# Channel mix of a four-layer block: LayerNorm output transposed by DMA in fp16 halves instead of by TensorE

## Chip, cores and metric

The kernel runs on one core of a Trainium2 chip. The metric is the device time of one execution in microseconds (us), the median of several runs.

## What is computed

A residual stream `x` of 8 sequences (batches) of 512 tokens and 512 features passes through four layers: a cosine cross attention, a ternary feed-forward network, a softmax cross attention, and a channel mix. The change touches only the last one, which adds to `x` the following function of its layer norm:

```python
x_prev = jnp.concatenate([jnp.zeros((B, 1, C), x.dtype), x[:, :-1, :]], axis=1)
xr = mu_r * x + (1.0 - mu_r) * x_prev
xk = mu_k * x + (1.0 - mu_k) * x_prev
r = jax.nn.sigmoid(jnp.einsum('btc,dc->btd', xr, W_r))
k = jnp.einsum('btc,dc->btd', xk, W_k)
k_act = jnp.square(jax.nn.relu(k))
out = r * jnp.einsum('btc,dc->btd', k_act, W_v)
```

Here `x` is the layer norm (no gain, no bias) of the stream, and `x_prev` is the same one token earlier. All products are taken in fp16 with a high and a low half for each operand, three matmuls for one product, so that the result is close to float32.

## The kernel before

The stream stays in SBUF for the whole program (`X`, 128 tokens on the partitions, four token tiles a batch). The four stages run one after the other; the channel mix (`channel_mix`, from L1867) is the last. In it each engine has a program of its own, written out by hand: a first batch, a loop over batches 1 to 6 (`batches`), and a last one. Semaphores are wrapped in `Tally`, so that `s.wait(e, b, k)` waits until k signals of batch b are there. An engine executes its program strictly in order.

While batch b is multiplied, batch b+1 is prepared:

- **VectorE** (`step`, L2021): statistics (L135), `bn_aggr`, the normalised tokens `z` (L147, after GpSimd's 1/sqrt at L161), then eight mixed rows `xf` (L2007, `mix`): four that feed the keys, and then four that feed the gates, each of these ahead of `gated` (L2014, `y` = values times gate) and `add` (L2019) of one token tile of batch b.
- **TensorE** (`step`, L2077): `keys(b)`, 4 x 12 matmuls; `ln_t`, which turns `z` of batch b+1 by 16 float32 transposes (L165), four for each 128-feature chunk, into two PSUM banks; `gates(b)`, 4 x 12 matmuls; `values(b)`, 4 x 12 matmuls. `values` of token tile 2 waits until `y` of tile 0 has freed its bank (L2072).
- **ScalarE** (`step`, L1981): for the keys a Relu, a Square and a copy to fp16 (L1969 to L1974); `transposed`, four copies of 128x512 from PSUM into `zf` (features on the partitions, tokens along them, one zero column first, L1946); then `part` (L1954, the previous-token term) and `xh` (L1962, the fp16 high half of a mixed row), with the four sigmoids (`gate`, L1979) between them.
- **GpSimd** (`step`, L1928): 1/sqrt, four low halves of the squared keys `kl` (L1926), and eight low halves of the mixed rows `xl` (L1920).
- **SyncE**: one store of 1 MB a batch (L1908).

The first key matmul of batch b+1 needs the four `xl` of the keys, the first gate matmul all eight.

Of the kernel before, what the change touches and what calls it, by code (L numbers as in the profile page):

```python
# [14 lines left out]
P = 128  # L15
# [14 lines left out]
class Tally:  # L30

    def __init__(self, sem, per, by=1):
        self.sem, self.per, self.by = sem, per, by

    def count(self, b, k):

        return b * (self.per * self.by) + k * self.by + 1

    def wait(self, eng, b, k):

        n = self.count(b, k)
        if isinstance(n, int) and n <= 1:
            return
        eng.wait_ge(self.sem, n)  # L46
        if not isinstance(n, int) and eng.engine in (mybir.EngineType.Pool, mybir.EngineType.DVE, mybir.EngineType.SP):
            eng.nop(nofuse=True)  # L48


def starts():


    each = lambda names, value: {n: value for n in names.split()}
    norm = lambda batch: each("st mv z", 1 + batch * TT) | each("ve rstd", 1 + batch) | each("T", 1 + batch * KD)
    a = each("hi lo bias const ws wp wm wt raw0 raw1", 0) | norm(0) | each(
        "x cf zh zl ch cl proj pf sq ph pl norm root rec nmr dot w y add", 1)
# [5 lines left out]
    m = each("hi lo raw", 0) | norm(1) | each("zf", 1 + KD) | each("part xf xh xl", 1 + KD) | each(  # L63
        "kp kf kk kh kl rp r vp y x out", 1)
    return dict(a=a, f=f, s=s, m=m)


def program(nc, x_d, ctx_d, wv_d, bv_d, wt_d, bt_d, w1_d, cw_d, cb_d, w2_d,
            wq_d, bq_d, wk_d, bk_d, wvv_d, bvv_d, wo_d, bo_d, wr_d, wkk_d, wvo_d, mur_d, muk_d, out_d):
    with ExitStack() as ctx:  # L70
# [7 lines left out]
        def tile(b, q):  # L78

            return X[:, bass.ds(b * (TT * D) + q * D, D)]  # L80

        sems = {stage: {n: ctx.enter_context(nc.semaphore(f"{stage}_{n}")) for n in names}
                for stage, names in starts().items()}
        env = dict(nc=nc, X=X, ident=ident, ones=ones, mhalf=mhalf, banks=banks, pairs=pairs, tile=tile, sems=sems)
        sm = lambda n, shape, dt=F32: ctx.enter_context(nc.sbuf_tensor("sm_" + n, shape, dt))
        env.update(zz=sm("zz", [P, 2 * KD * (S + 1)], F16), cx=sm("cx", [P, 4 * KD * S], F16),
# [1780 lines left out]
def channel_mix(env, wvo_d, out_d):  # L1867
# [3 lines left out]
    with ExitStack() as ctx:  # L1871
# [15 lines left out]
        T, KB, RB, VB = banks[0:2], banks[2:4], banks[4:6], banks[6:8]  # L1887

        s_hi, s_lo = sem("hi"), sem("lo")
        s_raw = [sem("raw")]  # L1890
        s_zf = tally("zf", KD)
# [4 lines left out]
        ln_v, ln_p, ln_t, s_T, s_z = norm_tools(env, a, sem, tally)  # L1896
# [4 lines left out]
        @block.sync  # L1901
        def _(e):
            ws(e)

            def store(b):
                s_x.wait(e, b, TT)
                s_out.wait(e, b, 0)
                e.dma_start(out_d[bass.ds(b, 1), :, :].rearrange("o (q p) d -> p (o q) d", p=P),  # L1908
                            X[:, bass.ds(b * (TT * D), TT * D)].rearrange("p (q d) -> p q d", d=D))\
                    .then_inc(s_out.sem, 16)  # L1910
            store(0)
            batches(e, 1, B, store)
            s_out.wait(e, B, 0)

        @block.gpsimd
        def _(e):
            def mixed(b, first=0):
                for i in range(first, 2 * KD):
                    s_xh.wait(e, b, i + 1)
                    e.tensor_tensor(xl[:, i, :], xf[:, i % 3, :], xh[:, i, :], ALU.subtract).then_inc(s_xl.sem, 1)  # L1920

            def squared(b):
                s_vp.wait(e, b, 0)
                for m in range(KD):
                    s_kh.wait(e, b, m + 1)
                    e.tensor_tensor(kl[:, m, :], kk[:, m % 3, :], kh[:, m, :], ALU.subtract).then_inc(s_kl.sem, 1)  # L1926

            def step(b, last):  # L1928
                if not last:
                    ln_p(e, b + 1)  # L1930
                squared(b)
                if not last:
                    mixed(b + 1)

            mixed(0, KD)
            step(0, False)
            batches(e, 1, B - 1, lambda b: step(b, False))
            step(B - 1, True)

        @block.scalar  # L1940
        def _(e):
            def transposed(b):
                s_xf.wait(e, b, 0)
                for c in range(KD):
                    s_T.wait(e, b, c + 1)
                    e.activation(zf[:, c, 1:S + 1], T[c % 2][:, :], ACT.Copy).then_inc(s_zf.sem, 1)  # L1946

            def mix(b, i, begun=0):

                if i < 2 * KD:  # L1950
                    c = i % KD
                    s_zf.wait(e, b, c + 1)
                    s_xf.wait(e, b, max(i - 1, begun))
                    e.activation(part[:, i % 2, :], zf[:, c, 0:S], ACT.Copy, scale=omu[:, i:i + 1])\  # L1954
                        .then_inc(s_part.sem, 1)
                if i > begun:
                    if i == 1:
                        s_kp.wait(e, b, 0)
                    if i == KD + 1:
                        s_rp.wait(e, b, 0)  # L1960
# [3 lines left out]
            def keys(b):  # L1964
                s_vp.wait(e, b, 0)
                for m in range(KD):
                    s_kk.wait(e, b, max(m - 1, 0))
                    s_kp.wait(e, b, m + 1)
                    e.activation(kf[:, m % 2, :], KB[m % 2][:, :], ACT.Relu, scale=1 / WS).then_inc(s_kf.sem, 1)  # L1969
                    s_kf.wait(e, b, m + 1)  # L1970
                    s_kl.wait(e, b, max(m - 2, 0))
                    e.activation(kk[:, m % 3, :], kf[:, m % 2, :], ACT.Square).then_inc(s_kk.sem, 1)  # L1972
                    s_kk.wait(e, b, m + 1)
                    e.activation(kh[:, m, :], kk[:, m % 3, :], ACT.Copy).then_inc(s_kh.sem, 1)  # L1974

            def gate(b, q):
                s_y.wait(e, b, 0)
                s_rp.wait(e, b, q + 1)
                e.activation(r[:, q, :], RB[q % 2][:, :], ACT.Sigmoid, scale=1 / WS).then_inc(s_r.sem, 1)  # L1979

            def step(b, last, first=False):  # L1981
                keys(b)
                if not last:
                    transposed(b + 1)
                if first:
                    wa(e)
                for q in range(TT):
                    if not last:
                        mix(b + 1, q)
                    gate(b, q)  # L1990
                if not last:
                    for i in range(TT, 2 * KD + 1):
                        mix(b + 1, i)

            for i in range(KD, 2 * KD + 1):
                mix(0, i, KD)
            step(0, False, True)
            batches(e, 1, B - 1, lambda b: step(b, False))
            step(B - 1, True)

        @block.vector
        def _(e):
            def mix(b, i):
# [37 lines left out]
        def _(e):  # L2041
# [85 lines left out]
```

## Time and profile before

| | |
|---|---|
| median of 3 runs | 1653.15 us (1650.3 to 1653.52) |
| the profiled execution | 1648.01 us, of which its span 1646.2 us |
| channel mix in it | from 1360.6 us to the end |
| one batch of it, start of keys to start of the next keys | 35.09 us |

The profile gives for one execution how long each engine was busy, what released it after a wait, and when each instruction started. A batch is the stretch from its first key matmul (1467.96 us for the batch shown below) to the next one's.

### The profile page before, as it was taken

How to read it: one execution, taken by the hardware profiler on the slowest of the kernel's cores; microseconds unless marked ns; L12 is line 12 of the kernel's file. 1: busy time of each engine (PE TensorE's matmuls, PEld its weight loads, DVE VectorE, ACT ScalarE, POOL GpSimd, SP SyncE). 2: the span in 40 equal slices, each digit the busy share in tenths (PEclk: the TensorE clock that was granted, in tenths of full speed). 3: DMA queues.
4: the chain of work that ended last, by engine and by line, in shares of the span. 5: the costliest groups of instructions: out<-in, count | busy, mean ns of one | idle time of the engine just before them, and what ended most of it. 6: DMA issues, size and time to landing. Idle time of an engine off the chain costs nothing. (4 is left out here: it accounts for less than half of the span.)

```text
span 1646.2 us, 28592 instructions
## 1 busy us (share of the span) xinstructions
PE 1495.9 (91%) x8836; PEld 672.5 (41%) x8836; DVE 1189.8 (72%) x1438; ACT 1116.6 (68%) x1895; POOL 1022.6 (62%) x738
## 2 busy tenths in 40 slices
PE   5989888998999984889999999999999969999998
PEld 3545433443444441334333434343434314444443
DVE  4989898988888764667686868676777756555562
ACT  6677598887888752667666767666766656666662
POOL 4777537766777732766677767677767565454442
PEclk9999999999999996999999999999999979999999
DMA  8321000000000023121121212121211200100001
GB/s 327 132 77 51 0 1 1 1 1 1 0 1 1 22 64 89 35 55 39 42 55 38 58 34 58 35 57 35 57 35 40 56 26 26 52 25 25 25 25 51
DMA packets 61225, 72.16 MB, mean 44 GB/s; under 512 B 15312, under 2 KB 40784, under 8 KB 60624
## 3 DMA queue, kind: packets, MB, share of 16 engines
q1 hardware_dynamic: 57968, 62.36, 12.9%
q10 hardware_dynamic: 3168, 8.78, 1.4%
q8 instruction: 36, 0.59, 0.2%
q14 instruction: 53, 0.43, 0.1%
HBM read 37.40 MB, written 8.39 MB: 28 GB/s over the span
## 5 line engine op out<-in xcount | busy, mean ns | idle before, releaser
L1607 DVE TENSOR_REDUCE s_mx<-bank 128x2 f32<-128x1024 f32 x256 | 301.0, 1218 | 176.0 <-PE bank L1733 175.2
L1483 ACT ACTIVATE s_E<-bank 128x512 f32<-128x512 f32 x512 | 281.5, 597 | 165.3 <-PE bank L1751 164.2
L1367 POOL TENSOR_TENSOR s_E<-s_E 128x1024 f32<-128x1024 f32 x128 | 302.7, 2376 | 79.8 <-ACT s_E L1483 79.0
L1751 PE MATMUL bank<-s_QA,s_KA 97*128 97x512 f16 x512 | 164.7, 385 | 21.6 <-DMA s_QA<-s_mrow 10.8
L1920 POOL TENSOR_TENSOR sm_cx<-m_xf,sm_cx 128x512 f16<-128x512 f32 x60 | 84.1, 1408 | 102.1 <-ACT sm_cx L1962 102.1
L1759 PE MATMUL bank<-s_E,s_V 128*32 128x512 f32 x1024 | 138.5, 613 | 4.8 <-ACT s_E L1483 2.9
L1611 DVE RECIPROCAL bank<-bank 128x256 f32<-128x256 f32 (+1 forms) x66 | 112.7, 1707 | 17.6 <-PE bank L1767 17.6
L1112 PE MATMUL bank<-f_w2q,w2raw 128*128 128x512 f16 x512 | 121.8, 379 | 0.6 <-DVE w2raw L964 0.3
L1089 PE MATMUL bank<-sm_zz,w1raw 128*128 128x512 f16 x256 | 100.6, 393 | 23.6 <-DVE sm_cx L976 13.4
L786 POOL TENSOR_TENSOR sm_wkv<-sm_wkv,sm_cx 128x511 f32<-128x511 f32 x48 | 66.2, 1379 | 89.0 <-DVE sm_wkv L976 79.6
L780 POOL TENSOR_TENSOR w1raw<-w1raw,sm_cx 128x512 f32<-128x512 f32 x88 | 115.8, 1338 | 2.3 <-ACT sm_cx L868 2.3
L2007 DVE SCALAR_TENSOR_TENSOR m_xf<-sm_zz,sm_mu,m_part 128x512 f32<-128x512 f32 x60 | 58.6, 978 | 75.9 <-ACT m_part L1954 74.9
L1089 PE MATMUL bank<-sm_wq,w1raw 128*128 128x512 f16 x256 | 97.2, 380 | 12.0 <-DVE sm_cx L976 7.7
L1090 PE MATMUL bank<-sm_zz,w1raw 128*128 128x512 f16 x256 | 100.3, 392 | 0.0
L1090 PE MATMUL bank<-sm_wq,w1raw 128*128 128x512 f16 x256 | 97.0, 379 | 0.0
L1751 PEld LDWEIGHTS bank<-s_QA,s_KA 97*128 97x128 f16 x512 | 41.1, 97 | 121.6 <-DVE s_mx L1607 72.4
L1360 POOL TENSOR_TENSOR sm_cx<-s_qkf,sm_cx 128x512 f16<-128x512 f32 x32 | 37.1, 1159 | 80.4 <-ACT sm_cx L1461 80.0
L1112 PEld LDWEIGHTS bank<-f_w2q,w2raw 128*128 128x128 f16 x512 | 49.9, 98 | 61.3 <-ACT w2raw L926 0.8
L1767 PE MATMUL bank<-s_E,ones 128*32 128x512 f32 x512 | 69.0, 612 | 5.3 <-POOL s_E L1367 5.3
L1360 POOL TENSOR_TENSOR sm_cx<-s_qkf,s_qkh 128x512 f16<-128x512 f32 x32 | 37.1, 1160 | 56.0 <-ACT s_qkh L1461 54.3
L1694 PE MATMUL bank<-sm_wkv,sm_cx 128*128 128x128 f16 x384 | 69.7, 220 | 0.8 <-DVE sm_wkv L197 0.8
L1696 PE MATMUL bank<-sm_wkv,sm_cx 128*128 128x128 f16 x384 | 69.3, 219 | 0.0
(268 smaller groups left out, 4031.3 us busy)
## 6 DMA issues: line engine op xcount, KB each, us to landing
sm_cx<-in_ctx SPq DMA_DIRECT2D x16, 768.0 KB, 4.6
X<-in_x SPq DMA_DIRECT2D x8, 1024.0 KB, 6.3
s_QA<-sm_cx SPq DMA_DIRECT2D x256, 32.0 KB, 1.9
out_x<-X SPq DMA_DIRECT2D x8, 1024.0 KB, 4.3
s_KA<-sm_cx SPq DMA_DIRECT2D x244, 32.0 KB, 1.9
w1raw<-in_w ACTq DMA_DIRECT2D x1, 4096.0 KB, 14.2
w2raw<-in_w ACTq DMA_DIRECT2D x1, 4096.0 KB, 27.2
s_QA<-s_qkh SPq DMA_DIRECT2D x128, 32.0 KB, 1.9
```

Of the source, the lines that this page charges most:

```text
L780: e.tensor_tensor(o, o, s2b[:, :], ALU.mult).then_inc(s_u.sem, 1)
L1089: e.matmul(hb(odd, j), w1q[:, cols], zh(odd, c), start=(c == 0), stop=False)
L1090: last = e.matmul(hb(odd, j), w1q[:, cols], zl(odd, c), start=False, stop=(c == KD - 1))
L1112: last = e.matmul(OB[q][:, :], whole16[:, r % NQ, q * P:(q + 1) * P, 0], w2q[:, ORDER[r] * D:(ORDER[r] + 1) * D], start=False, stop=(r == ...
L1360: e.tensor_tensor(qkl[:, w, :], qkf[:, :], qkh[m % 2][:, w, :], ALU.subtract).then_inc(s_qkl.sem, 1)
L1367: e.tensor_tensor(into, into, other, ALU.add).then_inc(s_sum.sem, 1)
L1483: e.activation(E[:, SLOT[k] + h, :], s_bank(u, nxt)[:, :], ACT.Exp, scale=1.0 / float(np.sqrt(DH)))\
L1607: e.tensor_reduce(mx[:, 2 * i:2 * i + 2, q], MAXED[i][:, :, :], AX.X, ALU.max).then_inc(s_red.sem, 1)
L1611: e.reciprocal(DEN[:, i * n:(i + 1) * n], DEN[:, i * n:(i + 1) * n]).then_inc(s_rc.sem, 1)
L1751: e.matmul(s_bank(u, nxt)[:, :], KA[0:MROW + 1, m, h, t * P:(t + 1) * P], QA[0:MROW + 1, m, h, :], start=True, stop=True).then_inc(s_sc.se ...
L1759: e.matmul(NUM[h * DH:(h + 1) * DH, :], V[:, m, t, h * DH:(h + 1) * DH], E[:, SLOT[t] + h, :], start=(t == 0), stop=(t == TT - 1)).then_in ...
L1920: e.tensor_tensor(xl[:, i, :], xf[:, i % 3, :], xh[:, i, :], ALU.subtract).then_inc(s_xl.sem, 1)
```

## The change

`z` is no longer transposed by TensorE. VectorE still writes it in float32. ScalarE copies each token tile to fp16 (`zth`), two tiles after key 2 and two after key 3; VectorE subtracts (`ztl = z - zth`); SyncE issues for each token tile two DMA transposes, of 128 tokens x 512 features in fp16, 128 KB each, SBUF to SBUF; and GpSimd adds the two turned halves into `zf` for one token tile at a time (`joined`). So `zf` is complete for any feature chunk only when all four token tiles are in; `mix` now waits for all four (`s_zf.wait(e, b, TT)`). ScalarE's four copies out of PSUM are gone, and its first `part` moves from ahead of gate 0 to behind gate 1. `values` and its wait for `y` are as they were. Six of the added counters use semaphores of the first stage again, from the value where that stage left them.

```diff
@@ sync @@
+            def transposed(b):
+                for q in range(TT):
+                    cols = slice(q * P, (q + 1) * P)
+                    s_zth.wait(e, b, q + 1)
+                    e.dma_start_transpose(zTh[:, :, cols], zth[:, q, :]).then_inc(s_zT[q].sem, 16)
+                    s_ztl.wait(e, b, q + 1)
+                    e.dma_start_transpose(zTl[:, :, cols], ztl[:, q, :]).then_inc(s_zT[q].sem, 16)
+            def step(b, last):
+                if not last:
+                    transposed(b + 1)
+                store(b)
@@ gpsimd @@
+            def joined(b):
+                s_xf.wait(e, b, 0)
+                for q in range(TT):
+                    s_zT[q].wait(e, b, 2)
+                    cols = slice(q * P, (q + 1) * P)
+                    e.tensor_tensor(zf[:, :, 1 + q * P:1 + (q + 1) * P], zTh[:, :, cols], zTl[:, :, cols], ALU.add)\
+                        .then_inc(s_zf.sem, 1)
                 squared(b)
                 if not last:
+                    joined(b + 1)
                     mixed(b + 1)
@@ scalar @@
-            def transposed(b):
-                s_xf.wait(e, b, 0)
-                for c in range(KD):
-                    s_T.wait(e, b, c + 1)
-                    e.activation(zf[:, c, 1:S + 1], T[c % 2][:, :], ACT.Copy).then_inc(s_zf.sem, 1)
+            def high(b, q):
+                s_z.wait(e, b, q + 1)
+                e.activation(zth[:, q, :], z[:, q, :], ACT.Copy).then_inc(s_zth.sem, 1)
-                    s_zf.wait(e, b, c + 1)
+                    s_zf.wait(e, b, TT)
+                    if m >= KD - 2 and not last:
+                        for q in range(2 * (m - KD + 2), 2 * (m - KD + 3)):
+                            high(b + 1, q)
                 for q in range(TT):
-                    if not last:
-                        mix(b + 1, q)
                     gate(b, q)
+                    if not last and q:
+                        mix(b + 1, q - 1)
                 if not last:
-                    for i in range(TT, 2 * KD + 1):
+                    for i in range(TT - 1, 2 * KD + 1):
                         mix(b + 1, i)
@@ vector @@
+            def low(b, q):
+                s_zth.wait(e, b, q + 1)
+                e.tensor_tensor(ztl[:, q, :], z[:, q, :], zth[:, q, :], ALU.subtract).then_inc(s_ztl.sem, 1)
-                    ln_v(e, b + 1)
+                    for q in range(TT):
+                        stats(e, b + 1, q)
+                    moments(e, b + 1)
+                    for q in range(TT):
+                        normalise(b + 1, q)
+                    for q in range(TT):
+                        low(b + 1, q)
@@ tensor @@
                 keys(b)
-                if not last:
-                    ln_t(e, b + 1, T, s_zf)
                 gates(b)
```

How the instructions stand now, where the time is decided. SyncE, the first batch of the stage, with what each waits for (`m_x` counts the finished token tiles of batch b; `a_w` and `a_y` are now the counters of the fp16 high and low halves of `z`). Before:

```order
L185 DMA m_stage<-in_wvo 128x4x512
L1908 DMA out_x<-X 128x4x512 [waits m_x]
L204 UNCONDITIONAL_BRANCH
L204 ISA
L46 ISA [waits m_x]
L1908 ISA [waits m_out]
L1908 DMA out_x<-X 128x4x512
```

And now:

```order
L194 DMA m_stage<-in_wvo 128x4x512
L1930 DMA_TRANSPOSE m_zTh<-m_zth 128x4x128 [waits a_w]
L1932 DMA_TRANSPOSE m_zTl<-m_ztl 128x4x128 [waits a_y]
...
L1922 DMA out_x<-X 128x4x512 [waits m_x]
L213 UNCONDITIONAL_BRANCH
L213 ISA
```

The pair of transposes stands there four times, one after another in one queue, ahead of the store.

ScalarE, the first batch, from the last key's Square on (`m_T` counts TensorE's transposed chunks, `m_zf` the writes of `zf`, `m_rp` the gate products). Before:

```order
L1972 ACTIVATE m_kk<-m_kf 128x512 [waits m_kl,m_kf]
L1974 ACTIVATE m_kh<-m_kk 128x512 [waits m_kk]
L1946 ACTIVATE sm_zz<-bank 128x512 [waits m_T,m_xf]
L1946 ACTIVATE sm_zz<-bank 128x512 [waits m_T] x3
L191 ACTIVATE m_wvh<-m_stage 128x2048 [waits m_raw]
L1954 ACTIVATE m_part<-sm_zz,sm_omu 128x512 [waits m_xf,m_zf]
L1979 ACT_TABLE_LOAD
L1979 ACTIVATE m_r<-bank 128x512 [waits m_rp]
L1954 ACTIVATE m_part<-sm_zz,sm_omu 128x512 [waits m_xf,m_zf]
L1962 ACTIVATE sm_cx<-m_xf 128x512 [waits m_xf,m_kp]
```

And now:

```order
L2008 ACTIVATE m_kk<-m_kf 128x512 [waits m_kl,m_kf]
L2010 ACTIVATE m_kh<-m_kk 128x512 [waits m_kk]
L1982 ACTIVATE m_zth<-m_z 128x512 [waits m_z] x2
L200 ACTIVATE m_wvh<-m_stage 128x2048 [waits m_raw]
L2018 ACT_TABLE_LOAD
L2018 ACTIVATE m_r<-bank 128x512 [waits m_rp] x2
L1990 ACTIVATE m_part<-sm_zz,sm_omu 128x512 [waits m_xf,m_zf]
L2018 ACTIVATE m_r<-bank 128x512 [waits m_rp]
L1990 ACTIVATE m_part<-sm_zz,sm_omu 128x512 [waits m_xf,m_zf]
L1998 ACTIVATE sm_cx<-m_xf 128x512 [waits m_xf,m_kp]
```

Two sigmoids now stand ahead of the first `part`, and the other two behind it.

GpSimd, the first batch (`a_add`, `a_dot`, `a_st` and `a_z` now count the landed transposes of token tiles 0 to 3). Before:

```order
L161 TENSOR_TENSOR m_rstd<-m_ve,mhalf 128x4 [waits m_ve]
L1926 TENSOR_TENSOR m_kl<-m_kk,m_kh 128x512 [waits m_kh] x4
L1920 TENSOR_TENSOR sm_cx<-m_xf,sm_cx 128x512 [waits m_xh] x8
L204 UNCONDITIONAL_BRANCH
L204 ISA
```

And now:

```order
L170 TENSOR_TENSOR m_rstd<-m_ve,mhalf 128x4 [waits m_ve]
L1955 TENSOR_TENSOR m_kl<-m_kk,m_kh 128x512 [waits m_kh] x4
L1962 TENSOR_TENSOR sm_zz<-m_zTh,m_zTl 128x4x128 [waits a_add,m_xf]
L1962 TENSOR_TENSOR sm_zz<-m_zTh,m_zTl 128x4x128 [waits a_dot]
L1962 TENSOR_TENSOR sm_zz<-m_zTh,m_zTl 128x4x128 [waits a_st]
L1962 TENSOR_TENSOR sm_zz<-m_zTh,m_zTl 128x4x128 [waits a_z]
L1949 TENSOR_TENSOR sm_cx<-m_xf,sm_cx 128x512 [waits m_xh] x8
```

The four joining adds stand between the low halves of the keys and those of the mixed rows.

## Rows read from the trace of the kernel before

**Rows 1.** The page, its first line
```profile
span 1646.2 us, 28592 instructions
```

**Rows 2.** Busy time by stretch: keys, transposes, the whole batch
```profile
core 0: us, PE busy (x) PEld busy (x) DVE busy (x) ACT busy (x) POOL busy (x), PEclk, DMA share, GB/s
1467.96:1478.32 10.36, 10.36 (x49) 4.60 (x47) 8.22 (x14) 6.21 (x10) 6.65 (x7) 1.00 0.27 101
1478.32:1482.33 4.01, 2.22 (x17) 1.76 (x17) 1.56 (x2) 3.23 (x6) 1.98 (x2) 1.00 0.00 0
...
1467.96:1503.05 35.09, 33.30 (x161) 15.73 (x160) 20.28 (x29) 21.36 (x36) 17.32 (x15) 1.00 0.08 30
```

**Rows 3.** Timeline of TensorE: start, us, engine, line, operation, [idle before <-releaser]
```profile
1478.10 0.38 PE L2047 MATMUL bank<-sm_cx,sm_wq 128*128 128x512 f16 x1
1480.01 1.09 PE L165 MATMUL bank<-ident,m_z 128*128 128x128 f32 x8 [1.53 <-DVE m_z L147]
1481.35 1.14 PE L165 MATMUL bank<-ident,m_z 128*128 128x128 f32 x8 [0.25 <-ACT sm_zz L1946]
```

**Rows 4.** Timeline of VectorE, one batch
```profile
1470.83 2.47 DVE L135 BATCH_NORM_STATS2 m_st<-X 128x6 f32 x4
...
1475.53 4.35 DVE L147 TENSOR_SCALAR m_z<-X,m_mv,m_rstd 128x512 f32 x4 [1.95 <-POOL m_rstd L161]
1483.98 0.75 DVE L2007 SCALAR_TENSOR_TENSOR m_xf<-sm_zz,sm_mu,m_part 128x512 f32<-128x512 f32 x1 [4.11 <-ACT m_part L1954]
...
1495.70 0.69 DVE L2014 SCALAR_TENSOR_TENSOR m_y<-bank,m_r 128x512 f32<-128x512 f32 x1 [0.62 <-PE bank L2047]
...
1499.85 1.65 DVE L2007 SCALAR_TENSOR_TENSOR m_xf<-sm_zz,sm_mu,m_part 128x512 f32<-128x512 f32 x1
```

**Rows 5.** Timeline of GpSimd, the same batch
```profile
1499.24 1.71 POOL L1920 TENSOR_TENSOR sm_cx<-m_xf,sm_cx 128x512 f16<-128x512 f32 x1 [2.02 <-ACT sm_cx L1962]
```

**Rows 6.** Groups of instructions, 1440 to 1610 us: count | busy us, mean ns | idle before
```profile
L1954 ACT ACTIVATE m_part<-sm_zz,sm_omu 128x512 f32<-128x512 f32 x40 | 28.5, 712 | 0.0
...
L1926 POOL TENSOR_TENSOR m_kl<-m_kk,m_kh 128x512 f16<-128x512 f32 x20 | 23.9, 1204 | 8.5 <-ACT m_kh L1974 8.5
...
L2019 DVE TENSOR_TENSOR X<-X,m_y 128x512 f32 x19 | 15.5, 818 | 3.8 <-DVE m_y L2014 3.8
...
L1979 ACT ACTIVATE m_r<-bank 128x512 f32<-128x512 f32 x20 | 11.9, 597 | 20.2 <-PE bank L2047 20.2
```

**Rows 7.** DMA view, 700 to 760 us: packets, queue, issues (KB each, us to landing)
```profile
DMA packets 3583, 2.98 MB, mean 50 GB/s; under 512 B 1136, under 2 KB 3193, under 8 KB 3577
...
q1 hardware_dynamic: 3577, 2.91, 18.2%
...
s_QA<-sm_cx SPq DMA_DIRECT2D x28, 32.0 KB, 1.9
```

**Rows 8.** DMA view, 1471 to 1505 us: the queue in one store
```profile
q1 hardware_dynamic: 528, 1.05, 8.2%
```

**Rows 9.** DMA view of the whole program: a load of 256 KB
```profile
s_bo<-in_bo SPq DMA_DIRECT2D x1, 256.0 KB, 3.2
```

**Rows 10.** Timeline of SyncE: copies issued in a row
```profile
704.00 7.50 SPq L1301 DMA_DIRECT2D s_QA<-sm_cx  x12
...
725.51 4.94 SPq L1301 DMA_DIRECT2D s_QA<-s_qkh  x8
```

**Rows 11.** Timeline of VectorE as the stage begins
```profile
1361.66 1.41 DVE L2007 SCALAR_TENSOR_TENSOR m_xf<-sm_zz,sm_mu,m_part 128x512 f32<-128x512 f32 x2 [1.39 <-ACT m_part L1954]
1363.72 2.69 DVE L2007 SCALAR_TENSOR_TENSOR m_xf<-sm_zz,sm_mu,m_part 128x512 f32<-128x512 f32 x2 [0.65 <-ACT m_part L1954]
```

**Rows 12.** Timeline of TensorE as the stage begins
```profile
1360.59 0.59 PE L2045 MATMUL bank<-sm_cx,sm_wq 128*128 128x512 f16 x1 [1.55 <-PEq L1206]
...
1365.24 0.63 PE L2047 MATMUL bank<-sm_cx,sm_wq 128*128 128x512 f16 x1
...
1366.31 0.38 PE L2047 MATMUL bank<-sm_cx,sm_wq 128*128 128x512 f16 x1
```

More of the change, by code:

```diff
@@ L30, with __init__ @@
 class Tally:
-    def __init__(self, sem, per, by=1):
-        self.sem, self.per, self.by = sem, per, by
+    def __init__(self, sem, per, by=1, base=0):
+        self.sem, self.per, self.by, self.base = sem, per, by, base
     def count(self, b, k):
-        return b * (self.per * self.by) + k * self.by + 1
+        return b * (self.per * self.by) + k * self.by + 1 + self.base
     def wait(self, eng, b, k):
         n = self.count(b, k)
-        if isinstance(n, int) and n <= 1:
+        if isinstance(n, int) and n <= 1 + self.base:
             return
@@ L62, in starts @@
         "shq0 shk0 shq1 shk1 shq2 shk2 shq3 shk3 md0 md1 md2 md3", 1)
-    m = each("hi lo raw", 0) | norm(1) | each("zf", 1 + KD) | each("part xf xh xl", 1 + KD) | each(
+    m = each("hi lo raw", 0) | norm(1) | each("zf", 1 + TT) | each("zth ztl", TT) | each("zT0 zT1 zT2 zT3", 2 * 16) | each("part xf xh xl", 1 + KD) | each(
         "kp kf kk kh kl rp r vp y x out", 1)
     return dict(a=a, f=f, s=s, m=m)
+AGAIN = (("m", "zth", "w"), ("m", "ztl", "y"), ("m", "zT0", "add"), ("m", "zT1", "dot"),
+         ("m", "zT2", "st"), ("m", "zT3", "z"))
 def program(nc, x_d, ctx_d, wv_d, bv_d, wt_d, bt_d, w1_d, cw_d, cb_d, w2_d,
@@ L80, in tile @@
             return X[:, bass.ds(b * (TT * D) + q * D, D)]
-        sems = {stage: {n: ctx.enter_context(nc.semaphore(f"{stage}_{n}")) for n in names}
+        again = {(stage, name) for stage, name, _ in AGAIN}
+        sems = {stage: {n: ctx.enter_context(nc.semaphore(f"{stage}_{n}")) for n in names if (stage, n) not in again}
                 for stage, names in starts().items()}
+        for stage, name, first in AGAIN:
+            sems[stage][name] = sems["a"][first]
         env = dict(nc=nc, X=X, ident=ident, ones=ones, mhalf=mhalf, banks=banks, pairs=pairs, tile=tile, sems=sems)
@@ L1879, in channel_mix @@
         zf = zz[:, :].bitcast(F32).rearrange("p (c s) -> p c s", s=S + 1)
+        zth, ztl = sb("zth", [P, TT, D], F16), sb("ztl", [P, TT, D], F16)
+        zTh, zTl = sb("zTh", [P, KD, S], F16), sb("zTl", [P, KD, S], F16)
+        z, mv, rstd = a["z"], a["mv"], a["rstd"]
         part, xf = sb("part", [P, 2, S]), sb("xf", [P, 3, S])
@@ L1886, in channel_mix @@
         wl = [wq[:, KD * D:], wkv[:, KD * D:2 * KD * D], sb("wvl", [P, KD * D], F16)[:, :]]
-        T, KB, RB, VB = banks[0:2], banks[2:4], banks[4:6], banks[6:8]
+        KB, RB, VB = banks[2:4], banks[4:6], banks[6:8]
         s_hi, s_lo = sem("hi"), sem("lo")
         s_raw = [sem("raw")]
-        s_zf = tally("zf", KD)
+        s_zf = tally("zf", TT)
+        s_zth, s_ztl = (Tally(sem(n), TT, 1, B * TT) for n in ("zth", "ztl"))
+        s_zT = [Tally(sem(f"zT{q}"), 2, 16, B * TT) for q in range(TT)]
         s_part, s_xf, s_xh, s_xl = (tally(n, 2 * KD) for n in ("part", "xf", "xh", "xl"))
@@ L1895, in channel_mix @@
         s_out = tally("out", 1, 16)
-        ln_v, ln_p, ln_t, s_T, s_z = norm_tools(env, a, sem, tally)
+        stats, moments, _, ln_p, _, _, _, s_z, s_rstd = norm_tools(env, a, sem, tally, parts=True)
         ws, wa, wvec = load_split([(wvo_d.rearrange("(c p) n -> p c n", p=P), stage[:, :], wh[2], wl[2])], s_raw, s_hi, s_lo)
@@ L1910, in store @@
                     .then_inc(s_out.sem, 16)
-            store(0)
-            batches(e, 1, B, store)
+            def transposed(b):
[9 more added lines that the diff above has]
+                store(b)
+            step(0, False)
+            batches(e, 1, B - 1, lambda b: step(b, False))
+            step(B - 1, True)
             s_out.wait(e, B, 0)
@@ L1962, in mix, with keys @@
                     e.activation(xh[:, i - 1, :], xf[:, (i - 1) % 3, :], ACT.Copy).then_inc(s_xh.sem, 1)
-            def keys(b):
+            def keys(b, last):
                 s_vp.wait(e, b, 0)
@@ L1981, in step @@
             def step(b, last, first=False):
-                keys(b)
-                if not last:
-                    transposed(b + 1)
+                keys(b, last)
                 if first:
@@ L2008, in mix, with normalise @@
                                        ALU.mult, ALU.add).then_inc(s_xf.sem, 1)
+            def normalise(b, q):
+                s_rstd.wait(e, b, 1)
+                e.tensor_scalar(z[:, q, :], tile(b, q), mv[:, q, 0:1], rstd[:, q:q + 1],
+                                ALU.subtract, ALU.mult).then_inc(s_z.sem, 1)
+            def low(b, q):
+                s_zth.wait(e, b, q + 1)
+                e.tensor_tensor(ztl[:, q, :], z[:, q, :], zth[:, q, :], ALU.subtract).then_inc(s_ztl.sem, 1)
             def gated(b, q):
```

1 line of the change is left out of this document (removed).

## The prediction, made before the changed kernel ran

> **What bounds the kernel now.** I read the page first, for the span of 1646.2 us [rows 1], and then the busy time by stretch inside the last stage. One batch lasts 35.09 us. TensorE is without a gap in its keys (10.36 us of 10.36), and the same holds for gates and values, which are as long: 3 x 10.36 = 31.08. Between keys and gates lies a slot of 4.01 us in which it is busy for 2.22 [rows 2]. So TensorE bounds the stage, and the slot is all that the transposes cost: it starts with a wait for `z`, then come 16 transposes in two groups, with a wait for ScalarE's copies between them [rows 3]. The other engines have room: ScalarE is busy 21.36 us, VectorE 20.28, GpSimd 17.32 [rows 2]. Seven batches are prepared this way (1 to 7), so without the slot at most 7 x 4.01 = 28 us are to be had.
>
> **But the slot is short because the path behind it is short.** The timeline of VectorE shows the cycle that has to be watched. A batch's statistics start at 1470.83, its last `z` ends at 1475.53 + 4.35 = 1479.88; the first `xf` starts 4.11 us later, after the transposes, at 1483.98; `y` of token tile 0 starts at 1495.70, after a wait for TensorE of 0.62 [rows 4]. VectorE does `xf` 0 to 4 before that `y`, and TensorE's third values product waits for that `y`. So if `zf` comes late, `xf` 4 comes late, then `y` 0, then values 2 and 3, then the next batch's statistics, for VectorE reaches these only after its last add. Before, `xf` 0 to 4 were spread out under the gates; this room is what the change spends.
>
> **The change part by part, from the start of a batch's statistics (D = 0) to the start of the next one's.**
> 1. Statistics, 1/sqrt and `z` are unchanged: 9.05 us (1479.88 - 1470.83) [rows 4].
> 2. The first `ztl`: a VectorE operation with two float32 operands took 818 ns [rows 6]; take 0.82. The first `zth` needs only the first `z` and a free ScalarE, so its transpose leaves while VectorE still writes `z`; the other seven follow the first `ztl` in one queue.
> 3. Seven more transposes at a spacing I, and the last one's landing L. No row shows a DMA transpose. Below: copies of 32 KB follow each other after 7.50 / 12 = 0.62 us [rows 10] and land after 1.9 [rows 7]. A load of 256 KB lands after 3.2 [rows 9], so 128 KB would be some 2.4 by these two. For the engines' part I count packets. In a store, 528 packets (2 KB each) take 8.2% of 16 engines x 34 us, 84.5 ns each [rows 8]. Between 700 and 760 us 3577 packets take 18.2% of 960 us; without 384 of the large kind (3577 - 3193) it is 142.3 us for 3193, of which 1136 are tiny and 2057 of 1 KB [rows 7]. Both together give a line of 25.6 ns a packet and 29.5 ns a KB. A transposed half is written in 128 x 4 runs of 256 B, 32 for each of 16 engines, at 33 ns: 1.06 us. At the mean of all packets in that stretch, 48.8 ns, it is 1.56. Above: one transpose waits until the one ahead has landed, 2.4 us. I take I = 1.2, between the two packet counts, and L = 2.4: 7 x 1.2 + 2.4 = 10.8 us.
> 4. The last joining add on GpSimd: like `kl`, 1.2 us [rows 6]. The other three lie under the transposes, behind `kl`.
> 5. From `zf` to `y` 0: `part` and five `xf` back to back. When the stage begins they come that way: the first four take from 1361.66 to 1366.41, 4.75 us, with GpSimd's `xl` between them, and a fifth adds 1.35 [rows 11]; 0.8 for the first `part` (0.71 [rows 6] and a handover), and two sigmoids of 0.6 [rows 6] that ScalarE now has between its parts, 1.2; and `y` itself, 0.7. Sum 8.8.
> 6. From the end of `y` 0 to the next statistics: 1495.70 + 0.69 = 1496.39 to 1470.83 + 35.09 = 1505.92, 9.5 us [rows 2, 4]. It was so long before as well, since VectorE and GpSimd slow each other here: `xf` took 1.65 instead of 0.75 while GpSimd's `xl` took 1.71 [rows 4, 5].
>
> Sum: 9.05 + 0.82 + 10.8 + 1.2 + 8.8 + 9.5 = 40.2 us a batch, against 35.09: 5.1 more, 7 times, 36 us. The profiled execution took 1648.0 (span 1646.2 and 1.8 around it), which would become 1684; the median of the runs lies 5 above it, so **1689 us**.
>
> Hidden parts: TensorE's 4.01 us are saved on an engine that then waits some 9 us a batch before values 2. Its clock may fall there from 2.4 to 1.2 GHz: at the stage's start, behind a pause, it ran at the lower level, 0.63 us a matmul instead of 0.38, from 1360.59 to about 1366 [rows 12], which at half speed loses 2.8 us. These lie beside item 6, since VectorE needs longer for `y` 1 and `y` 2 than TensorE for two products; uncovered they would be 7 x 2.8 = 20 us. ScalarE's four fp16 copies a batch take the place of its four copies from PSUM and move ahead of the gates, where it has time. The store now stands behind the transposes of the next batch in SyncE's queue, but its own wait comes later than they do.
>
> A rule on the price itself: the Trainium skill, VectorE: DVE Perf Modes, section "The three transpose paths", puts 128x128 in bf16 at 390 ns on TensorE and 1309 ns by DMA. Read as an estimate for the spacing (1.3 instead of 1.2) it gives 40.9 us a batch and 7 x 5.8 = 41 us more. No row here can confirm it.
>
> **The rivals.**
> - *The forecast: the transposes' queue lengthens VectorE's cycle.* For I from 0.62 with L = 1.9 (35.6 us, +4) to 1.56 with L = 2.4 (42.7 us, +53): 1657 to 1706. Chance 0.72.
> - *Slower still, up to one transpose at a time.* From I = 1.56 on; I = 2.4 gives 29.4 + 16.8 + 2.4 = 48.6 us a batch, +94, 1748. For it: none of the copies shows two-byte elements scattered over partitions. Against: copies overlap freely, twelve in 7.50 us with a landing time of 1.9 each [rows 7, 10]. Chance 0.14.
> - *The transposes are cheap, and TensorE gives back its slot: faster.* The queue decides below 7 I + L = 35.09 - 29.37 = 5.7 us. If they cost nothing beyond the last `ztl` (three more of 0.82 after the first) and a landing of 1.9: 9.05 + 3.28 + 1.9 + 1.2 + 8.8 + 9.5 = 33.7, -10 us, 1643; if items 5 and 6 shrink too, TensorE's 31.1 us are the floor, -28 us, 1625. For it: ScalarE is idle for 13.7 of 35.09 us and VectorE for 14.8 [rows 2]. Against: it needs a spacing below the 0.62 of the plainest copies. The Trainium skill, Advanced Engine Details and Errata, "X-Bar Transpose (TRN2)", says that transposes are as fast as regular DMAs; by that rule this case, or the lower end of the first, would come. Chance 0.09.
> - *The two cancel within 0.2%.* Chance 0.05.
>
> **How the numbers follow.** A measurement here tells about 0.2%, 3.3 us, from no change. The range of 1650 to 1740 us leaves out the cheap case (0.09) and about half of the slow one (0.07). The likeliest case's own range is 1657 to 1706. Faster 0.09, the same 0.05, slower 0.86.
>
> **What would show it.** Right: a batch of about 40 us; TensorE idle some 9 us in one piece before the third values product, released by VectorE's `y`; the first `part` released by GpSimd's last joining add, and this by a DMA; eight transposes on SyncE's queue at even spacing, the last issued some 8 us after the first `ztl`; half clock behind the pause. Wrong: if the gates follow the keys and the values the gates with no gap at all, or if the last transpose lands within 6 us of the first `ztl`; or if the pause lies elsewhere, such as before keys, which would mean that GpSimd's adds, not the queue, set the time.

## The result, and the profile of the changed kernel

The changed kernel takes 1680.6 us (median of 4 runs, 1679.34 to 1681.84), the kernel before beside it 1651.74 us (4 runs, 1650.3 to 1653.52): a ratio of 1.0174, 95% interval 1.0157 to 1.0192, or 28.9 us more. The profiled executions differ by 1677.5 - 1646.2 = 31.3 us of span [rows 1].

The first line of the page, and the busy time by stretch: a batch from its first statistics on VectorE to the next one's, and one from its first key matmul on TensorE to the next one's:

```profile
span 1677.5 us, 28615 instructions
```

```profile
core 0: us, PE busy (x) PEld busy (x) DVE busy (x) ACT busy (x) POOL busy (x), PEclk, DMA share, GB/s
1483.67:1523.23 39.56, 32.84 (x142) 14.29 (x141) 25.10 (x33) 20.88 (x36) 23.26 (x19) 0.91 0.21 53
1480.47:1520.72 40.25, 33.53 (x145) 14.57 (x144) 25.79 (x34) 21.29 (x36) 23.95 (x19) 0.92 0.20 52
```

A batch lasts 39.56 us where it took 35.09 [rows 2], with every engine idle for at least 6.7 of them: no engine bounds the stage, a chain through several does. The batch shown is the shortest of the steady ones: behind the first, five spacings of the first statistics are 39.56 to 40.16 us, 39.80 in the mean, against 35.16 in the mean before. Seven times 4.64 are 32.5; the stage's first statistics start 1.5 earlier in this execution (1364.81 against 1366.34), which leaves 31, the difference of the spans. The stores show the same spacing, since each waits for the last add of its batch (timeline of SyncE's queue; before each store stand the eight transposes, left out here):

```profile
1444.43 0.41 SPq L1922 DMA_DIRECT2D out_x<-X  x1
...
1484.11 0.39 SPq L1922 DMA_DIRECT2D out_x<-X  x1
...
1523.68 0.39 SPq L1922 DMA_DIRECT2D out_x<-X  x1
...
1563.44 0.39 SPq L1922 DMA_DIRECT2D out_x<-X  x1
```

VectorE's timeline of that batch answers to [rows 4]:

```profile
1483.67 2.47 DVE L144 BATCH_NORM_STATS2 m_st<-X 128x6 f32 x4
...
1488.22 4.36 DVE L2049 TENSOR_SCALAR m_z<-X,m_mv,m_rstd 128x512 f32 x4 [1.80 <-POOL m_rstd L170]
1492.50 3.45 DVE L2054 TENSOR_TENSOR m_ztl<-m_z,m_zth 128x512 f16<-128x512 f32 x4
1506.04 0.75 DVE L2044 SCALAR_TENSOR_TENSOR m_xf<-sm_zz,sm_mu,m_part 128x512 f32<-128x512 f32 x1 [10.09 <-ACT m_part L1990]
...
1509.85 2.74 DVE L2044 SCALAR_TENSOR_TENSOR m_xf<-sm_zz,sm_mu,m_part 128x512 f32<-128x512 f32 x2 [0.38 <-ACT m_part L1990]
1512.52 0.68 DVE L2060 SCALAR_TENSOR_TENSOR m_y<-bank,m_r 128x512 f32<-128x512 f32 x1
...
1522.62 0.69 DVE L2065 TENSOR_TENSOR X<-X,m_y 128x512 f32 x1 [0.20 <-DVE m_y L2060]
1523.23 1.88 DVE L144 BATCH_NORM_STATS2 m_st<-X 128x6 f32 x3
```

The wait ahead of the first `xf` grew from 4.11 to 10.09 us. It is a wait for ScalarE's first `part`, this one waits for GpSimd's last join, and the join for a transpose (timelines of GpSimd and ScalarE):

```profile
1503.80 1.15 POOL L1962 TENSOR_TENSOR sm_zz<-m_zTh,m_zTl 128x512 f32<-128x512 f16 x1 [1.52 <-DMA m_zTl<-m_ztl]
1505.08 0.72 ACT L1990 ACTIVATE m_part<-sm_zz,sm_omu 128x512 f32<-128x512 f32 x1 [8.21 <-POOL sm_zz L1962]
```

What fills the wait is in the chain of work that ended last (start, us, what; the highs `zth` of SyncE are L1930, the lows L1932):

```profile
1492.58 0.61 DVE m_ztl L2054
1493.25 1.19 SPq L1932
1494.61 1.19 SPq L1930
...
1499.95 1.19 SPq L1930
1501.23 2.44 DMA m_zTl<-m_ztl
1503.81 1.16 POOL sm_zz L1962
```

From there it goes on through ScalarE's parts and sigmoids to `y` 0, and from `y` 0 to TensorE, whose timeline shows the idle piece and the clock behind it:

```profile
1513.25 0.61 PE L2097 MATMUL bank<-m_wvh,m_kh 128*128 128x512 f16 x1 [6.72 <-DVE m_y L2060]
...
1517.50 0.58 PE L2098 MATMUL bank<-m_wvl,m_kh 128*128 128x512 f16 x1
1517.92 0.38 PE L2099 MATMUL bank<-m_wvh,m_kl 128*128 128x512 f16 x1
...
1520.72 0.38 PE L2097 MATMUL bank<-sm_cx,sm_wq 128*128 128x512 f16 x1
```

TensorE waits 6.72 us in one piece ahead of its third values product (4.82 to 6.72 in the seven batches). Keys, gates and the first two values products are without a gap. From keys to keys its batches last 38.7 to 40.3 us; the lower clock behind the pause lasts for 8 to 14 matmuls.

### The profile page after: what moved, and what is told of

Same layout as the page of the kernel before. It is cut to its first block and busy times, and to the rows that moved or that the text cites. A ratio compares the mean times of both kernels' runs of the same rounds, so it can differ in the third digit from the quotient of the medians.

```text
span 1677.5 us, 28615 instructions
## 1 busy us (share of the span) xinstructions
PE 1492.7 (89%) x8724; PEld 663.2 (40%) x8724; DVE 1226.2 (73%) x1466; ACT 1115.4 (66%) x1895; POOL 1062.5 (63%) x766
## 5 line engine op out<-in xcount | busy, mean ns | idle before, releaser
L1760 PE MATMUL bank<-s_QA,s_KA 97*128 97x512 f16 x512 | 164.7, 385 | 21.6 <-DMA s_QA<-s_mrow 10.8
L2044 DVE SCALAR_TENSOR_TENSOR m_xf<-sm_zz,sm_mu,m_part 128x512 f32<-128x512 f32 x60 | 71.1, 1187 | 77.6 <-ACT m_part L1990 77.0
L1949 POOL TENSOR_TENSOR sm_cx<-m_xf,sm_cx 128x512 f16<-128x512 f32 x60 | 90.0, 1514 | 55.6 <-ACT sm_cx L1998 55.6
L2097 PE MATMUL bank<-m_wvh,m_kh 128*128 128x512 f16 x128 | 55.3, 432 | 42.1 <-DVE m_y L2060 42.1
L1990 ACT ACTIVATE m_part<-sm_zz,sm_omu 128x512 f32<-128x512 f32 x60 | 42.6, 711 | 57.6 <-POOL sm_zz L1962 53.1
```

Of the source, the lines that this page charges most:

```text
L1760: e.matmul(s_bank(u, nxt)[:, :], KA[0:MROW + 1, m, h, t * P:(t + 1) * P], QA[0:MROW + 1, m, h, :], start=True, stop=True).then_inc(s_sc.se ...
L2097: e.matmul(bank, wide_h(c), tall_h(c), start=(c == 0), stop=False)
```

## Experiments

Each median stands beside one of the kernel before, run on the same chip: 1649.41 us (24 runs) for the first four, 1651.14 (9 runs) for the next three, 1652.11 (24 runs) for the last four. "Batch" is the steady spacing of the first statistics in the profile (35.08 to 35.40 before; with the change 39.56 in the batch shown above, up to 40.16 in others).

| kernel | us | ratio to before, 95% | batch, us |
|---|---|---|---|
| 1 one DMA a token tile | 1659.25 | 1.0051 (1.0033 to 1.0069) | 36.5 to 36.8 |
| 2 high halves only | 1651.86 | 1.0006 (0.9991 to 1.0022) | 35.52 |
| 3 no transpose | 1648.40 | 0.9991 (0.9974 to 1.0008) | 34.75 |
| 4 idle matmuls | 1676.51 | 1.0163 (1.0131 to 1.0194) | 39.56 |
| 5 kernel before, parts later | 1683.34 | 1.0192 (1.0168 to 1.0217) | 40.2 to 40.9 |
| 6 two batches ahead | 1661.22 | 1.0070 (1.0044 to 1.0096) | 34.4 to 37.3 |
| 7 the same, one DMA a tile | 1658.83 | 1.0054 (1.0033 to 1.0075) | 34.4 to 37.4 |
| 8 statistics ahead | 1648.91 | 0.9975 (0.9959 to 0.9991) | 34.3 |
| 9 8, one DMA, parts earlier | 1647.25 | 0.9974 (0.9956 to 0.9993) | 34.13 |
| 10 kernel before, statistics ahead | 1642.69 | 0.9939 (0.9918 to 0.9961) | 33.33 |
| 11 all gates ahead of parts | 1681.07 | 1.0165 (1.0133 to 1.0196) | 39.4 to 39.6 |

### What a transpose costs

**1.** High and low half of a token tile lie side by side and go in one DMA of 128x1024, four DMAs instead of eight, with the same bytes.

```diff
-                    s_zth.wait(e, b, q + 1)
-                    e.dma_start_transpose(zTh[:, :, cols], zth[:, q, :]).then_inc(s_zT[q].sem, 16)
                     s_ztl.wait(e, b, q + 1)
-                    e.dma_start_transpose(zTl[:, :, cols], ztl[:, q, :]).then_inc(s_zT[q].sem, 16)
+                    e.dma_start_transpose(zT[:, :, cols], zhl[:, q, :]).then_inc(s_zT[q].sem, 16)
```

> One DMA transpose of 128 x 1024 a token tile (both halves, 256 KB) in place of two of 128 x 512; it waits for the low half. Theory (a fixed time of the queue, about 1.33 us for each transpose, whatever its size here): after the first low half three more transposes follow instead of six, 4 us a batch less, 7 x 4 = 28, so about 1652 us. Rival (the time goes by bytes, 1.33 us for 128 KB): a spacing of 2.7 us, and the first high half can't leave early: 1680 to 1690 us.

It comes close: 7 us above what was expected, and by the ratios some 20 us below the changed kernel. A batch is some 3 us shorter and not 4, as the larger transposes land 1.0 us later. SyncE's queue in this kernel, then its DMA view from 1471 to 1505 us; under each, the same two of the changed kernel:

```profile
1486.70 5.52 SPq L1931 DMA_TRANSPOSE m_zT<-m_zhl  x4
```

```profile
q1 hardware_dynamic: 4752, 2.10, 24.9%
...
m_zT<-m_zhl SPq DMA_TRANSPOSE x4, 3.4
```

```profile
1498.56 1.21 SPq L1932 DMA_TRANSPOSE m_zTl<-m_ztl  x1
1499.95 1.19 SPq L1930 DMA_TRANSPOSE m_zTh<-m_zth  x1
1501.23 1.21 SPq L1932 DMA_TRANSPOSE m_zTl<-m_ztl  x1
```

```profile
DMA packets 4880, 2.10 MB, mean 62 GB/s; under 512 B 4368, under 2 KB 4368, under 8 KB 4880
...
q1 hardware_dynamic: 4880, 2.10, 23.9%
...
m_zTl<-m_ztl SPq DMA_TRANSPOSE x4, 2.4
```

A transpose of 128x512 holds the queue for 1.2 us, and they follow at 1.28 to 1.39, 1.33 in the mean. One of 128x1024, with twice the bytes, holds it for 1.24 to 1.27; the four start at a spacing of 1.42 ((5.52 - 1.25) / 3), and land after 3.4 instead of 2.4. The engines' own time comes from the packets: without the store's 528 and its 8.2% [rows 8], the eight small ones are 4352 packets in 15.7% of 16 x 34 us, 19.6 ns each, 544 / 16 x 19.6 ns = 0.67 us a transpose. The four large ones are 4224 packets in 16.7%, 21.5 ns each, 1.42 us a transpose. So with 128x512 the DMA engines are half idle and the queue sets the pace, and with 128x1024 the engines are just full: the spacing is their own time, and a still wider transpose would gain nothing in bytes.

**2.** Only the high halves are transposed (behind the same wait for `ztl`), and GpSimd adds them to themselves; the low halves' part of `z` is left out.

```diff
-                    e.dma_start_transpose(zTl[:, :, cols], ztl[:, q, :]).then_inc(s_zT[q].sem, 16)
...
-                    e.tensor_tensor(zf[:, :, 1 + q * P:1 + (q + 1) * P], zTh[:, :, cols], zTl[:, :, cols], ALU.add)\
+                    e.tensor_tensor(zf[:, :, 1 + q * P:1 + (q + 1) * P], zTh[:, :, cols], zTh[:, :, cols], ALU.add)\
```

> The transposes of the low halves are left out and GpSimd adds the high half twice; everything else stays, each transpose waits for its tile's low half. Theory (queue of transposes): four issues at 1.33 us from the first low half on instead of seven in all, the last one leaves 4 us earlier: 35.6 us a batch, about 1652 us. If the transposes are not what sets the time: 1680 us.

As expected, and 35.52 us a batch is 4.04 below the changed kernel for four transposes fewer. Four take 5.27 us on the queue here.

**3.** No transpose at all. GpSimd adds the halves as they lie, so that `z` goes on unturned; everything else stays.

```diff
-                if not last:
-                    transposed(b + 1)
                 store(b)
...
-                    s_zT[q].wait(e, b, 2)
+                    s_ztl.wait(e, b, q + 1)
```

> No transposes at all: GpSimd adds the two fp16 halves as they lie, once the low half is there; nothing is turned. Theory: last low half 12.3 us after the statistics start, join 1.3, mixing up to y of tile 0 8.1, the rest 10.0: 31.8 us a batch against TensorE's floor of 31.1, so 7 x (31.8 - 39.6) = -54, about 1626 us. Rival (the added copies and subtractions on ScalarE and VectorE or the joining adds carry half of the loss): above 1645 us.

A clear miss: 34.75 us a batch, not some 32. The timelines of this kernel's VectorE and GpSimd show what comes next when the transposes cost nothing:

```profile
1480.72 4.41 DVE L2054 TENSOR_TENSOR m_ztl<-m_z,m_zth 128x512 f16<-128x512 f32 x4
```

```profile
1481.67 1.35 POOL L1953 TENSOR_TENSOR m_kl<-m_kk,m_kh 128x512 f16<-128x512 f32 x1 [1.60 <-ACT m_kh L2010]
1482.98 5.38 POOL L1960 TENSOR_TENSOR sm_zz<-m_zth,m_ztl 128x512 f32<-128x512 f16 x4
```

The four joining adds, hidden under the transposes before, now stand in a row for 5.38 us behind `kl` 3, and VectorE's lows cost 4.41. So, by the batches shown, the transposes account for 39.56 - 34.75 = 4.81 us, all that was lost and 0.34 more; the lows and joins by themselves use up what TensorE's slot gives back, and without any DMA the loop is as long as before, to 0.34 us.

### Which wait passes it on

**4.** Is the clock a part of it? 28 matmuls without use are put into TensorE's pause, ahead of the third values product.

```diff
+                    if q == 2 and not last:
+                        for i in range(28):
+                            e.matmul(banks[i % 2], kh[:, i % KD, 0:P], wh[2][:, 0:D], start=True, stop=True)
```

> The changed kernel with 28 unused matmuls of 512 columns on TensorE in the pause ahead of the third values product, into two banks that the stage no longer uses. Theory: the clock stays at 2.4 GHz and values 2 takes 2.6 instead of 4.7 us, but VectorE's chain from y of tile 0 to the next statistics is 10 us long anyway: the same time, 1677 to 1682 us. Rival (the lost clock is on the path): 7 x 2.1 = 15 us faster, 1666 us.

The busy time by stretch of this kernel:

```profile
1481.45:1521.01 39.56, 37.47 (x173) 16.60 (x172) 25.12 (x33) 21.34 (x37) 23.28 (x19) 1.00 0.21 53
```

Full clock throughout (1.00 instead of 0.91), and the same 39.56 us here; in the mean of five spacings it is 39.57 against 39.80. So what the lower clock costs lies beside VectorE's tail, but for 0.2 us a batch. Of the 4.9 us between the profiled executions, 2.1 stand before the added matmuls first run (the first statistics start at 1362.74 against 1364.81), so the edit did not bring them; 1.0 lies in the six spacings that follow. The last batch holds 1.8: no batch is prepared beside it, TensorE is without a gap, and it takes 37.6 and 37.5 us from its keys to the end. With the pause filled, these keys start 4.7 us ahead of the store before them, and 2.8 in the changed kernel. There the lost clock is on the path.

**5.** The change also moves ScalarE's first `part`. In the kernel before, with its transposes on TensorE, only that is moved, behind gate 1.

```diff
                 for q in range(TT):
-                    if not last:
-                        mix(b + 1, q)
                     gate(b, q)
+                    if not last and q:
+                        mix(b + 1, q - 1)
```

> The kernel before with one part of the change: ScalarE's first part moves behind gate 1, and the following ones by one place. Theory (late zf, not the order, costs the time): the first part could start at about 20.4 us after the keys' start, behind gate 1, and y of tile 0 ends 8.1 later, at 28.5, against 28.4 before: 0 to 4 us slower, 1652 to 1656. Rival (the order alone pushes the mixing into the values): over 1665 us.

Missed: this alone costs 32 us, as much as the whole change. ScalarE of this kernel:

```profile
1500.38 0.60 ACT L1946 ACTIVATE sm_zz<-bank 128x512 f32<-128x512 f32 x1 [0.26 <-PE bank L165]
1503.79 0.60 ACT L1979 ACTIVATE m_r<-bank 128x512 f32<-128x512 f32 x1 [2.81 <-PE bank L2047]
1506.38 0.60 ACT L1979 ACTIVATE m_r<-bank 128x512 f32<-128x512 f32 x1 [1.99 <-PE bank L2047]
1506.88 0.71 ACT L1954 ACTIVATE m_part<-sm_zz,sm_omu 128x512 f32<-128x512 f32 x1
```

On TensorE the transposes stand ahead of the gates. So `zf` is ready at 1500.98, but `part` waits for gate 1, which is 5.9 us later; VectorE's first `xf`, `y` 0, the adds and the next statistics follow, and the next `z` is later still. It is the same loop by another door: the order of the change would be wrong with TensorE's transposes, and it says nothing of the cost of the move in the changed kernel, where the gates don't wait for `z`. There the first `part` starts at 1505.08 after 8.21 us of waiting for GpSimd's last join, and gate 1 has ended at 1496.87: its place behind gate 1 costs nothing.

**11.** The other two sigmoids still stand between the parts. Here, in the changed kernel, all four stand ahead of the first `part`.

```diff
                     gate(b, q)
-                    if not last and q:
-                        mix(b + 1, q - 1)
                 if not last:
-                    for i in range(TT - 1, 2 * KD + 1):
+                    for i in range(2 * KD + 1):
                         mix(b + 1, i)
```

> The changed kernel with all four sigmoids ahead of the first part on ScalarE, while it waits for the transposes anyway. Theory (item 5 of the prediction: two sigmoids of 0.5 to 0.6 lie between the parts): about 1 us a batch less, 7 to 8 us, about 1673 us. If VectorE and GpSimd set the pace of the mixing: the same as the changed kernel, 1680.

Missed: nothing is gained. The two sigmoids between the parts, 1.2 us in item 5 of my sum, don't set the pace of the mixing.

### Taking the transposes out of the loop

**6, 7.** Everything up to the transposes is done two batches ahead, so that a batch's transposes have 35 us; in 7 with the edit of 1 as well. ScalarE's parts also go back to their place before the change, and GpSimd joins between the first and the second `kl`. The core of it, on SyncE and on ScalarE, whose highs now wait until the batch before has been joined:

```diff
-            def step(b, last):
-                if not last:
-                    transposed(b + 1)
+            def step(b, ahead):
+                if ahead:
+                    transposed(b + 2)
                 store(b)
...
+                        if m == KD - 2 and not (isinstance(nxt, int) and nxt == 1):
+                            s_zf.wait(e, nxt - 1, TT)
```

> The changed kernel with the normalised tokens, halves and transposes of batch b+2 made in batch b, while GpSimd joins those of batch b+1; ScalarE's parts are ahead of the gates as in the kernel before. Theory (only the latency of the queue in VectorE's cycle costs time): the cycle is open, TensorE's 31.1 us a batch is the floor; batch 0 stays at some 40, batch 1 at some 34, the other five at 31 to 32: about 1638 us (1630 to 1648), faster than before. Rival (VectorE, busy 25 of 39.6 us and slowed by GpSimd, or GpSimd bound the stage): no batch under 34, 1648 us or more.

> The same with one transpose of 128 x 1024 a token tile. Theory: in the steady batches the queue's time no longer matters, so it gains only in batches 0 and 1, 4 to 8 us in all if e1_pair gained: about 1632 us; if e1_pair did not gain, the same as e6_ahead.

Missed, both. The table of waits of 6, 1440 to 1630 us (engine, what waited <- for what: us, times, longest):

```profile
ACT m_zth L1992 <- POOL sm_zz L1965: 15.5, 4, 3.9
...
PE bank L2134 <- ACT m_r L2030: 12.8, 4, 3.2
```

The wait for the DMA is gone, and my own new wait has taken its place: the highs stand between the keys' products on ScalarE and stop until GpSimd has joined, then the last Relu, and behind it the first sigmoids, are late. That 7 is not clearly better than 6 (by 2.4 us, and their intervals overlap) fits: the DMA no longer matters there.

**8.** Only statistics and 1/sqrt of batch b+2 are done ahead, in VectorE's pause; highs two after each of keys 0 and 1.

```diff
                     for q in range(TT):
-                        stats(e, b + 1, q)
-                    moments(e, b + 1)
-                    for q in range(TT):
                         normalise(b + 1, q)
...
+                    if not (isinstance(b, int) and b == B - 2):
+                        measured(b + 2)
                     for i in range(KD):
```

> The changed kernel with the statistics and 1/sqrt of batch b+2 made in VectorE's pause of batch b (while it waits for the transposes) instead of at the start of the next step; ScalarE's fp16 copies go behind keys 0 and 1. The transposes are untouched. Theory (the loop add - statistics - z - transposes - mixing - y sets the time): the 4.55 us from the first statistics to the first z leave the loop, 39.6 - 4.55 = 35.05 us a batch, 7 x 4.55 = 32 less, about 1649 us. Rival (the queue's wait alone counts, and GpSimd or ScalarE now hold it): above 1665 us.

As expected. With the eight transposes untouched, a batch falls from 39.56 to 34.3 us, 0.7 more than the 4.55 of the statistics; in the batch from 1513.93 us on, `z` took 3.53 us instead of 4.36. The loop was too long by what could be taken out of it elsewhere.

**9.** 8 with one DMA a token tile and each `part` one place earlier (the first diff). **10.** The same idea without the change: the kernel before, statistics ahead, ScalarE's copies from PSUM ahead of key 3 (the second diff).

```diff
-                    s_zth.wait(e, b, q + 1)
-                    e.dma_start_transpose(zTh[:, :, cols], zth[:, q, :]).then_inc(s_zT[q].sem, 16)
...
-                    if not last and q:
-                        mix(b + 1, q - 1)
+                    if not last:
+                        mix(b + 1, q)
```

```diff
                 if not last:
-                    ln_v(e, b + 1)
+                    normalise(e, b + 1)
...
+                    if m == KD - 1 and not last:
+                        transposed(b + 1)
```

> The same with one transpose of 128 x 1024 a token tile, and ScalarE's parts one place earlier (gate 0, part 0, gate 1, ...). Theory: the pair took 2.9 us a batch from the loop in e1_pair, the statistics take 4.55: 39.6 - 7.4 = 32.2 us a batch, a little over TensorE's 31.1: 7 x 7.4 = 52 less than the changed kernel, about 1628 us (1622 to 1638), faster than the kernel before by 1.2%. Rival (VectorE and GpSimd, which slow each other, bound the stage at some 34): 1642 us or more.

> The kernel before, with TensorE's transposes, and the same early statistics; ScalarE copies the transposed chunks ahead of key 3 instead of behind it. Theory: TensorE no longer waits 1.5 us for z in its slot, 7 x 1.5 = 10 us faster than before, about 1641 us; its slot of 2.3 to 2.5 us for the transposes stays, so e9_best is still ahead. If TensorE waits for the copies instead: 1648 to 1651.

9 missed by 19 us. GpSimd in 9, then TensorE:

```profile
1488.02 1.16 POOL L1954 TENSOR_TENSOR m_kl<-m_kk,m_kh 128x512 f16<-128x512 f32 x1 [0.65 <-ACT m_kh L2011]
1489.13 4.47 POOL L1961 TENSOR_TENSOR sm_zz<-m_zT 128x512 f32<-128x512 f16 x4
```

```profile
1494.99 0.39 PE L2104 MATMUL bank<-sm_wkv,sm_cx 128*128 128x512 f16 x1 [2.50 <-ACT m_r L2019]
```

The joins stand in a row behind `kl` 3, as in 3, and the second sigmoid behind the first `part` that waits for them, so the gates now wait. 10 came as expected and has the lowest median of all, 9.4 us under the kernel before, where 9 had been expected to be ahead of it. Its busy time by stretch:

```profile
1479.87:1513.20 33.33, 33.08 (x162) 15.81 (x160) 19.70 (x29) 21.24 (x37) 18.33 (x14) 1.00 0.09 32
```

TensorE is busy for 33.08 of 33.33 us, its transposes among them. The slot of 4.01 us [rows 2] had some 1.8 of waiting in it, and that was to be had without the change.

## Why the prediction was right

It said 1689 us; 1680.6 were measured. The sum gave 40.2 us a batch, and 39.56 came. Item by item, from the rows of the changed kernel above:

- **1 and 2**, statistics to the first `ztl`: 9.87 predicted; SyncE took the first low half at 1493.25, 9.58 after 1483.67.
- **3**, the queue and the landing: 10.8 predicted, 10.55 measured (1493.25 to 1503.80, when the last join starts), but by two errors that cancelled. After the first low half six more transposes follow, not the seven that I counted; and the spacing is 1.33, not 1.2. Six by 1.33 is 7.98, and the last takes 2.57 until GpSimd starts, against 2.4. The reason that I gave for the spacing fell as well: I took it from packets of 33 to 49 ns, and they take 19.6. It is the issue in the queue, 1.2 us, that sets it (1). That the item came out within 0.25 us is luck.
- **4**, the last join: 1.2 predicted, 1.28 with the handover (1503.80 to 1505.08).
- **5**, to the end of `y` 0: 8.8 predicted, 8.12 measured (1505.08 to 1513.20). Taking the two sigmoids out from between the parts gained nothing (11), so the 1.2 us for them were too much.
- **6**, to the next statistics: 9.5 predicted, 10.03 measured.

The profiled execution took 1679.34 where the sum gave 1684. Part of these 4.7 us are batches, which the sum made 0.4 too long against the mean of 39.80 (0.64 against the one shown): seven times, 2.6. Another 1.5 are the earlier start of the stage, which has nothing to do with the sum. The last 4 us are the step from one execution to the median, for which I added 5 and which was 1.3 here.

The wait that I named decides: VectorE's `y` 0 late, then the third values product. The signs ahead of it stood as well: `part` released by the last join, this by a DMA, and the last transpose issued 7.98 us after the first low half, where I had said some 8. I expected some 9 us of idle TensorE. From keys to keys its batch is 40.25, 9.17 longer than its 31.08, and of this 6.72 are idle and 2.45 (33.53 - 31.08) are lost to the half clock, since after the pause the clock stood at 1.2 GHz (0.61 to 0.63 us a matmul from 1513.25 on) and at 2.4 GHz (0.38) from 1517.92. I had put that loss at 2.8, and that it is hidden was right for the batches in which the next one is prepared, but for 0.2 us, and not for the last one (4).

The Trainium skill, VectorE: DVE Perf Modes, section "The three transpose paths", gives 1309 ns for a transpose of 128x128 by DMA. The spacing of 1.33 us agrees in size, but here for four such blocks, and 1.42 for eight; at this size it is nearly a price for each DMA. The Trainium skill, Advanced Engine Details and Errata, section "X-Bar Transpose (TRN2)", calls transposes as fast as regular DMAs. The traces do not agree. By the packets, 128 KB of a transpose took the DMA engines 0.67 us, and an eighth of the 1 MB store 528 x 84.5 ns / 16 / 8 = 0.35 us [rows 8]; and by the pace, plain copies of 32 KB followed each other at 0.62 us [rows 10].

What I had not seen is how little the change itself could have brought. I gave a chance of 0.09 to cheap transposes and a faster kernel, with 1643 us. In 3 they are free, and the time is that of the kernel before, within its interval; its batch of 34.75 us is 1.05 above the rival's 33.7. The rival charged 3.28 + 1.9 + 1.2 = 6.38 us from the last `z` to the last join. In 3 it is 1488.36 - 1480.80 = 7.56 without any landing: it counted one join behind the transposes, and with free ones four stand in a row behind `kl` 3. The loop of VectorE beyond that point is another 18.3 us (to 1506.64), whatever the transposes cost.

Open: since the queue sets the pace, two queues would be the next step. It was not tried, being not free of races: the Trainium skill, Advanced Engine Details and Errata, section "X-Bar Transpose (TRN2)", says that transposes in flight from two streams spoil each other's output. No run here shows it. Whether GpSimd's joins ahead of `kl` 1 to 3, in kernel 9, would reach TensorE's 31.1 us was not tried either.

## What to carry to other kernels

Before a step is taken off the busiest engine, add up the loop that it closes: here VectorE's last add, statistics, `z`, the turn, the mix, `y` and again the add. Before the change it fitted the batch with well under a microsecond to spare (0.62 us of wait for TensorE at `y` 0 [rows 4]), so a longer way round is paid in every batch, nearly in full, even on engines that are idle a third of the time. Look first for work on that loop which can be done earlier (statistics and 1/sqrt, 1488.22 - 1483.67 = 4.55 us a batch): in the changed kernel that took 5.3 us off a batch, more than the 4.5 that the exchange had added, and with TensorE's transposes kept it gave the lowest time. And when DMA transposes are on such a loop, make them few and wide: here up to 128x1024, at which the DMA engines were full.

## What the runs showed of the hardware

- A DMA transpose of 128x512 fp16 occupied the issuing queue for 1.2 us and one of 128x1024 for 1.25; in a row they followed at 1.33 and 1.42, and landed after 2.4 and 3.4 us. Plain copies of 32 KB followed at 0.62 [rows 10].
- A transpose moved its 128 KB in 544 packets of under 512 B, at 19.6 ns each (21.5 in the 128x1024 ones); a store's packet of 2 KB took 84.5 ns [rows 8]. By bytes the transposes took the DMA engines about twice as long as the store.
- GpSimd's joining add took 1.16 us beside an idle VectorE and 5.38 / 4 = 1.35 beside VectorE's lows, which took 4.41 us for four where they took 3.45 in the changed kernel.
- After a pause of 6.72 us TensorE ran at 1.2 GHz for 4.7 us (1513.25 to 1517.92). In the seven batches the pauses were 4.82 to 6.72 us and 8 to 14 matmuls ran at the lower level, not in the order of the pauses: 8 after 5.85 us, 14 after 6.11. With the pause filled the clock stayed at 2.4 GHz, and the batch shown was as long.
